# Attention stage of a two-layer graph network: another order of a tick's steps on four engines, and one add over two PSUM banks

## The reference

```
feat = concat([x[src], edge_weights, x[dst]], axis=1)
h = relu(feat @ W_att1.T + b_att1)
scores = (h @ W_att2.T + b_att2)[:, 0]
m = segment_max(scores, src)
e = exp(scores - m[src])
denom = segment_sum(e, src)
alpha = e / denom[src]
msg = segment_sum(alpha[:, None] * lin_x[dst], src)
```

## The kernel before

| engine | order |
|---|---|
| POOL | kl(k), r and splits(k-2), z d(k-4), maximum(k-3), W(k-4) |
| ACT | parts s(k-2), cr(k-4), p(k-4), PT copy(k-2), S(k), STb(k) |
| PE | mm(k-4), MK(k-3), pre(k-1), turn of parts(k-2), turn of C_N(k), ag(k-5) |
| DVE | acc(k-6), mg(k-4), maximum(k-3), acc(k-6), running maximum(k-3), C_N(k), two adds(k-1), scores(k-1) |

## Time and profile before

### The profile page before, as it was taken

The page is one execution under the profiler, slowest core; times in us unless marked ns, Lnnn a source line. Parts: engine busy times, 40 slices in busy tenths (PEclk is TensorE's granted clock), DMA queues, the critical chain, the costliest instruction groups (busy, mean ns, idle before and its releaser), DMA issues.

```text
span 7883.6 us, 169485 instructions
## 1 busy us (share of the span) xinstructions
PE 4875.0 (62%) x30913; PEld 3631.3 (46%) x30914; DVE 4538.2 (58%) x19982; ACT 2058.9 (26%) x5709; POOL 5047.4 (64%) x9951
## 2 busy tenths in 40 slices
PE   6333666566533475555555555555568888888887
PEld 3333333333333454444434444444446666666665
DVE  5666677677532482332323233232369999999997
ACT  4000000000000052222222222222235555555555
POOL 1666666666666446666666666666668878878886
PEclk9555555555555586667676666676689999999999
DMA  7222222222222224323222222222243443443443
GB/s 257 46 49 50 46 48 48 48 48 48 48 51 50 41 71 126 96 92 95 92 90 89 89 91 90 89 90 91 89 125 102 103 102 101 103 102 101 102 103 97
DMA packets 1160316, 670.13 MB, mean 85 GB/s; under 512 B 797187, under 2 KB 1060948, under 8 KB 1159396
## 3 DMA queue, kind: packets, MB, share of 16 engines
q1 hardware_dynamic: 1020628, 422.54, 21.8%
q0 software_dynamic: 137728, 243.98, 10.7%
q10 hardware_dynamic: 1888, 2.83, 0.1%
HBM read 371.08 MB, written 311.42 MB: 87 GB/s over the span
## 4 chain that ended last, share of the span: by engine, by line
another core or an unknown queue 15%; issue 15%; POOL 11%; PE 6%; DMA 4%; DVE 4%; ACT 3%; SPq 2%; DVEq 1%; POOLq 1%; ACTq 0%
PE banks L1402 4%; DMA wide<-rows_by_src 3%; POOL ring L875 2%; SPq L723 2%; ACT ring L1091 1%; ACT ring L1098 1%; POOL rows_by_src L841 1%; POOL ring L899 1%; DVE wide L2011 1%; POOL ring L893 1%; DVE wide L2016 1%; POOL ring L885 1%; DMA rows_by_src<-ring 1%; POOL ring L869 1%
## 5 line engine op out<-in xcount | busy, mean ns | idle before, releaser
L841 POOL DMA_INDIRECT rows_by_src<-ring x1760 | 1704.4, 968 | 1055.8 <-issue 517.8
L813 POOL DMA_INDIRECT wide<-msg_table,ring x1664 | 1576.5, 947 | 1062.8 <-issue 558.9
L1402 PE MATMUL banks<-wide,ring 128*128 x3520 | 1348.1, 513 | 938.1 <-ACT ring L1091 650.3
L1402 PEld LDWEIGHTS banks<-wide,ring 128*128 128x128 f32 x3520 | 793.7, 278 | 1192.2 <-issue 1150.2
L1316 PE MATMUL banks<-wide,ring 128*128 x3520 | 860.1, 426 | 680.0 <-DVE ring L1814 339.0
L1316 PEld LDWEIGHTS banks<-wide,ring 128*128 128x128 f32 x3520 | 784.9, 328 | 759.2 <-issue 758.7
L1098 ACT COPY ring<-banks 128x416 f32<-128x416 f32 x880 | 405.8, 518 | 1855.9 <-remote 1217.3
L1974 DVE COPY ring<-ring 128x4 f32<-128x4 f32 x440 | 81.8, 186 | 1353.0 <-DMA rows_by_src<-ring 1092.4
L1779 DVE TENSOR_TENSOR acc<-acc,banks 128x64 f32 x1760 | 389.2, 221 | 787.9 <-issue 269.1
L1443 PE MATMUL banks<-wide,ring 128*128 x5616 | 741.9, 282 | 2.2 <-ACT ring L1135 2.1
L1443 PEld LDWEIGHTS banks<-wide,ring 128*128 128x128 bf16 x5616 | 492.7, 98 | 160.5 <-issue 4.1
(11 more groups left out here) (334 smaller groups left out, 9797.6 us busy)
## 6 DMA issues: line engine op xcount, KB each, us to landing
wide<-rows_by_src SPq DMA_DIRECT2D x1872, 105.0 KB, 2.0
ring<-attr_turned SPq DMA_DIRECT2D x440, 128.0 KB
attr_turned<-ring SPq DMA_DIRECT2D x416, 96.0 KB
rows_by_src<-ring POOLq DMA_INDIRECT x1760
wide<-msg_table,ring POOLq DMA_INDIRECT x1664
ring<-attr_by_dst SPq DMA_DIRECT2D x208, 64.0 KB
attr_turned<-ring SPq DMA_DIRECT2D x208, 64.0 KB
attr_by_dst<-in_edge_attr_dram SPq DMA_DIRECT2D x1, 13281.2 KB
```

Source lines behind the costliest of these rows:

```text
L813: g.indirect_dma_start(out=A_g[:, b * GV + u, :], out_offset=None, in_=table[:, :], in_offset=bass.IndirectOffsetOnAxis(ap=A_idx[:, b * GV ...
L841: g.indirect_dma_start(out=rows_d[:, :], out_offset=bass.IndirectOffsetOnAxis(ap=B_pos[:, s, u:u + 1], axis=0), in_=B_row[:, s, u, :], in_ ...
L1402: mm(b, B_DT[:, t, u, :], qh[:, w, :].rearrange("p a k -> p (a k)"), start=True, stop=False)
```

## The change

The order of a tick is written anew on POOL, ACT, PE and DVE, and the two adds become one over both banks.

| engine | order after |
|---|---|
| POOL | wait for s(k-2), W(k-5), kl(k), r and splits(k-2), maximum(k-3), z d(k-4) |
| ACT | p(k-5), parts s(k-2), cr(k-4), S(k), PT copy(k-2), STb(k) |
| PE | MK(k-3), pre(k-1), mm(k-4), turn of parts(k-2), turn of C_N(k), ag(k-5) |
| DVE | acc(k-6), maximum(k-3), acc(k-6), running maximum(k-3), C_N(k), one add(k-1), mg(k-4), scores(k-1) |

p and W move from stage 4 to stage 5, so POOL and ACT have six stages instead of five. `pre` is waited for as a whole (`c_pre` of both banks), and `c_add` counts once a tick. mm waits for the running maximum too (`c_new`), whose operand lies in the bank that mm writes.

On POOL:

```
             def tick(i, s, stages):
+                if 2 in stages:
+                    after_c(pool, c_s, *stages[2], incs=2)
+                if 5 in stages:
+                    t, j = stages[5]
+                    after_c(pool, c_p, t, j)
+                    after_c(pool, c_ag, t, j, 2)
+                    g.tensor_tensor(C_W[:, t % 2, :, :], C_V[:, t, :, H1:ROW_SRC],
+                                    per_group(C_p[:, t, :], HID + 1), ALU.mult).then_inc(c_W, 1)
                 if 0 in stages:
...
                 if 2 in stages:
...
-                    after_c(pool, c_s, t, j, incs=2)
                     after_c(pool, c_pt, t, j, CS)
...
-                if 4 in stages:
-                    t, j = stages[4]
-                    after_c(pool, c_mg, t, j)
-                    after_c(pool, c_p, t, j, CS)
-                    ch.link(g.tensor_tensor(C_z[:, t, :], C_s[:, t, :], C_mg[:, t, :], ALU.subtract))
-                    turn(pool, "pool")
-                    g.tensor_scalar(C_d[:, t, :], C_z[:, t, :], 0.0, None, ALU.min).then_inc(c_d, 1)
                 if 3 in stages:
...
                 if 4 in stages:
                     t, j = stages[4]
-                    after_c(pool, c_p, t, j)
-                    after_c(pool, c_ag, t, j, 2)
-                    g.tensor_tensor(C_W[:, t % 2, :, :], C_V[:, t, :, H1:ROW_SRC],
-                                    per_group(C_p[:, t, :], HID + 1), ALU.mult).then_inc(c_W, 1)
-            run_ticks(pool, tick, 5, ch, CS * (2 + 1 + 4), CS, C_LOOPS)
+                    after_c(pool, c_mg, t, j)
+                    after_c(pool, c_p, t, j, CS)
+                    ch.link(g.tensor_tensor(C_z[:, t, :], C_s[:, t, :], C_mg[:, t, :], ALU.subtract))
+                    turn(pool, "pool")
+                    g.tensor_scalar(C_d[:, t, :], C_z[:, t, :], 0.0, None, ALU.min).then_inc(c_d, 1)
+            run_ticks(pool, tick, 6, ch, CS * (2 + 1 + 4), CS, C_LOOPS)
```

On ACT (S also moves ahead of the PT copy):

```
             def tick(i, s, stages):
+                if 5 in stages:
+                    t, j = stages[5]
+                    after_c(act, c_d, t, j)
+                    after_c(act, c_W, t, j, CS)
+                    a.activation(C_p[:, t, :], C_d[:, t, :], ACT.Exp).then_inc(c_p, 1)
                 if 2 in stages:
...
                     a.activation(C_cr[:, t, :], C_df[:, t, :], ACT.Exp).then_inc(c_cr, 1)
-                    after_c(act, c_d, t, j)
-                    after_c(act, c_W, t, j, CS)
-                    a.activation(C_p[:, t, :], C_d[:, t, :], ACT.Exp).then_inc(c_p, 1)
```

On PE the four small matmuls of mm stand behind `pre`:

```
+                if 4 in stages:
+                    t, j = stages[4]
+                    after_c(pe, c_mn, t, j)
+                    after_c(pe, c_mg, t, j, 1)
+                    if 3 in stages:
+                        after_c(pe, c_new, *stages[3])
+                    for u in range(GV):
+                        last = mm(bank[5][:, u * PARTS:(u + 1) * PARTS], C_STb[:, t, u, :], C_mp[:, t, u // 2, :], start=True, stop=True)
+                    last.then_inc(c_mm, 1)
```

On DVE, where mg also moves between the add and the scores:

```
-                def add_parts(half):
-                    c = slice(2 * half, 2 * half + 2)
-                    v.tensor_tensor(C_V[:, t1, c, 0:H1], two(bank[2 + half], H1), C_V[:, t1, c, 0:H1], ALU.add).then_inc(c_add, 1)
+                def add_parts():
+                    rows4 = C_V[:, t1, :, 0:H1].rearrange("p (h u) k -> p h u k", h=2)
+                    pre4 = by_window(2)[:, :, 0:2 * H1].rearrange("p h (u k) -> p h u k", u=2)
+                    v.tensor_tensor(rows4, pre4, rows4, ALU.add).then_inc(c_add, 1)
...
-                    dve.wait_ge(c_pre, (j1 * CS + t1) * 2 + 1)
-                    add_parts(0)
-                    dve.wait_ge(c_pre, (j1 * CS + t1) * 2 + 2)
-                    add_parts(1)
...
+                    after_c(dve, c_pre, t1, j1, incs=2)
+                    add_parts()
```

More of the change, by code:

```diff
@@ L1129, in tick @@
                 if 0 in stages:
-                    after_c(act, c_N, s, i)
-                    after_c(act, c_ag, s, i, CS)
-                    a.activation(C_S[:, s, :, :], C_N[:, s, :, :], ACT.Identity, bias=ones[:, 0:1], scale=-1.0).then_inc(c_S, 1)
                     after_c(act, c_St, s, i)
@@ L1135, in tick @@
                     a.activation(C_STb[:, s, :, :], four(bank_b[0], P), ACT.Identity, bias=ones[:, 0:1], scale=-1.0).then_inc(c_STc, 1)
-            run_ticks(act, tick, 5, None, 0, CS, C_LOOPS)
+            run_ticks(act, tick, 6, None, 0, CS, C_LOOPS)
             act.wait_ge(n_ones, 1)
@@ L1417, in tick @@
                     r = regs(ENG.PE, wpair_of, j1 * (C_BODY // 2) + t1 * PV, N_WIN - 1, PV)
-                if 4 in stages:
-                    t, j = stages[4]
-                    after_c(pe, c_mn, t, j)
-                    after_c(pe, c_mg, t, j, 1)
-                    for u in range(GV):
-                        last = mm(bank[5][:, u * PARTS:(u + 1) * PARTS], C_STb[:, t, u, :], C_mp[:, t, u // 2, :], start=True, stop=True)
-                    last.then_inc(c_mm, 1)
                 if 3 in stages:
@@ L2053, in tick @@
                     after_c(dve, c_s, t1, j1, CS, incs=2)
-                    dve.wait_ge(c_pre, (j1 * CS + t1) * 2 + 1)
-                    add_parts(0)
-                    dve.wait_ge(c_pre, (j1 * CS + t1) * 2 + 2)
-                    add_parts(1)
-                    dve.wait_ge(c_add, (j1 * CS + t1) * 2 + 1)
-                    score(0)
-                    score(1)
-                    dve.wait_ge(c_add, (j1 * CS + t1) * 2 + 2)
-                    score(2)
-                    score(3)
+                    after_c(dve, c_pre, t1, j1, incs=2)
+                    add_parts()
+                if 4 in stages:
+                    t4, j4 = stages[4]
+                    after_c(dve, c_mm, t4, j4)
+                    after_c(dve, c_d, t4, j4, CS)
+                    v.tensor_reduce(C_mg[:, t4, :], bank[5][:, 0:GV * PARTS].rearrange("p (u k) -> p u k", k=PARTS), AX.X, ALU.add).then_inc(c_mg, 1)
+                if 1 in stages:
+                    after_c(dve, c_add, t1, j1)
+                    for u in range(GV):
+                        score(u)
                 if 3 in stages and t3 == CS - 1:
```

11 lines of the change are left out of this document (5 added, 6 removed).

## The result

The changed kernel takes **8103.34 us** (median of four runs from 8094.83 to 8109.66) against 7887.37 us: a ratio of **1.0274, 95% interval 1.0256 to 1.0292**, or 216 us slower. The profiled execution has a span of 8107.7 us. The forecast was 8075, its range 7925 to 8170.

A forecast was written before the change was run, and what follows sets the result against it. Bound before: GpSimd's in-order queue, 4.215 us a tick. New loop: 3.88 + 0.44 + 0.28 + 0.02 = 4.62 us; +0.405 us times 468 = +190 us on 7885.51, so 8075 us, range 7925 to 8170.

The forecast's parts named there:

- The circle: Closed loop from GpSimd's W through d, ScalarE's p, parts and s, back to W: 3.88 us undisturbed, 4.62 with stalls.
- C_N's block: VectorE's C_N holds up GpSimd's first split once a tick, adding 0.44 us to the loop.
- s to GpSimd: Loop term from the start of ScalarE's s to GpSimd's start with W: 0.36 us.
- the penalties' 0.02: GpSimd's copy of penalties, one more small step of 0.14 us in every sixth tick: 0.02 us a tick.
- The scores' stall: VectorE's scores delay four GpSimd steps, the last of the maximum and z, by 0.07 each: 0.28 us, lower bound 0.
- The hand-over: On ScalarE from p to parts, shown in no row: taken as 0.20 us, with 0.11 as the other end.
- VectorE's room: From kl's start scores end at 2.60 us and d at 3.23, so VectorE has 0.6 us to spare.
- The signs announced: Parts behind p, W waiting 0.7 us for s, first split 0.62, VectorE under 82%, score 0.30, some 390 ticks.
- Faster: Rival: the loop through VectorE sets the pace, row load binding at 4.05 us a tick; 77 us less, 7808; chance 0.09.
- W's new neighbours: GpSimd's W runs away from the scores, giving VectorE back 0.21 us a tick, spare time worth nothing.
- the new place of mm and mg: TensorE's matmuls for the maximum behind the source part, mg behind the add: nothing on the loop, free while TensorE's 3.56 us fit.

The follow-up runs named there:

- s_at_r: Changed kernel with GpSimd's wait for s moved back in front of r, all else as changed: 7877.95 us, ratio 0.9996 to the kernel before.
- p_behind_s: Changed kernel with the exponential p behind parts and s on ScalarE instead of ahead of them: 7996.49 us, ratio 1.0144 to the kernel before.
- one_add: Kernel before with only the merged add, one operation over both banks in place of two: 7909.1 us, ratio 1.0029 to the kernel before.
- two_adds: Changed kernel with the add taken apart into two, both behind the wait for both banks: 8040.39 us, ratio 1.0196 to the kernel before.

## Why the prediction was right, point by point

**The circle** is what sets the tick: the trace shows it closed, and s_at_r shows that to open it at one place returns everything. Term by term, forecast (without the scores' 0.28) and mean of 385 ticks by starts: W to kl 0.58 and 0.58; kl to its follower 0.14 and 0.15; r to the second split with C_N's block 1.00 and 0.95; to the next 0.15 and 0.22; six steps of the maximum 0.88 and 1.03; to z 0.15 and 0.20; z to d 0.41 and 0.46; d to p 0.25 and 0.28; p to parts 0.20 and 0.18; parts to s 0.20 and 0.20; s to GpSimd 0.36 and 0.40. The sum is 4.67 with the penalties' 0.02, against 4.62. Times 468 the measured 0.45 us make 212 of the 216 us.

**C_N's block** was forecast at 0.44 on the first split and is 0.39 there (0.588 us for 0.20 in the group row), with 0.06 more on the second split, on which C_N falls in 71 ticks (0.260 for 0.20 on the mean). **The scores' stall** was forecast at four steps of 0.07, 0.28 in all, and is smaller: 0.15 in the steps of the maximum and 0.05 from z to d, 0.20 in all. What grew in front of z is something else, which the forecast put at nothing: z's wait for mg, 15.4 us in 386 ticks or 0.04 a tick, from the slow pres. So the forecast's size comes out as well as it does partly because a stall taken too long stands beside a wait and hand-overs taken too short. **The hand-over** p to parts, for which no row existed, was taken at 0.20 and is 0.18. **s to GpSimd** was 0.04 short: W waits here where r did before. **VectorE's room** was counted too wide: the 0.03 us from kl to C_N stands in no row of before; C_N starts 0.40 behind kl's start, the scores 1.87 and not 1.62, and on the mean they still end ahead of d.

**The signs announced** came: W's wait for s 0.83 (0.7), first split 0.588 (0.62), score 311 ns (0.30), VectorE 81% busy (under 82%), 386 ticks (390), parts released by p.

**The rivals.** Faster needed d ahead of the scores' end, and parts start 0.57 us (mean) after that end. The forecast valued the merged add, W's new neighbours and the new place of mm and mg at nothing; s_at_r, where all of them stand and the time is that of before, bears this out for them together. One by one it is not so: the add alone costs 23 us in the kernel before and 63 in the changed one, and mg's new place lets a slow pre reach z. The step that was wrong is "beside a loop that VectorE is not part of, all of this is worth nothing": VectorE is not part of it, but when its operations start decides which of the loop's steps are held up.

**The kernel before** is not GpSimd's chain alone, as the forecast read it off two ticks. Over 5900 to 7700 us the row loads and their issue hold 19% of its chain of waits, and kl waits for them in 161 of 427 ticks:

```profile
POOL ring L859 <- DMA wide<-rows_by_src: 55.8, 161, 0.9
```

The forecast does not suffer by it, since it adds the difference of two ticks' lengths, and 4.215 was counted.

**What the forecast did not see** is which of the two edits matters. It put p at the head first and the wait of W second; the runs reverse that. p at the head with the wait at r is as fast as before, and the wait alone, with p in its old place, is already slower by 166 us.

## What to carry to other kernels

Follow a result from the engine that makes it through every instruction queued behind it, until you are back at its maker: if a whole tick's steps lie on that circle, busy shares say nothing, and the length of the circle is the tick. Put a wait directly in front of the first instruction that needs the result; one step further ahead, W and kl, which needed nothing of s, were put on the circle, for 216 us. And before an order is changed, note what each moved step releases: W released the row loads, and kl ahead of it made the slowest kernel here.

## What the runs showed of the hardware that was not expected

- TensorE's granted clock fell from 2.4 to 1.2 GHz for 3.4 us after TensorE had stood still for 1.33 us inside a busy stretch (p_behind_s); the twelve pre matmuls then took 2.85 instead of 1.59 us. It happened in 32 of 384 ticks of the changed kernel, after pauses of 1.02 to 1.26 us, in 119 of 372 where it was worst, and in none before. A kernel that makes TensorE wait can so lose a second time. The pause alone does not decide it: of 227 pauses of at least 1.0 us in the changed kernel 195 brought no fall, and the eight falls of one_add came after 0.5 us.
- One add over two PSUM banks with 576 columns takes 0.752 us, two of 288 columns 0.45 each, started so that they overlap. Where the first score waits for its own half only, it comes 0.05 us earlier with two; where it waits for both (two_adds), 0.06 later.
- A longer VectorE row made the changed kernel no slower (0.28 us more a tick) or faster (0.06 us more, with two adds).
